# Eight-tile cross-attention and ternary FFN kernel: transposes of p moved to DMA, shared scale steps, new engine orders

## The reference, cut to what matters

```python
def xattn(h, ctx, Wq, bq, Wk, bk):            # h = layernorm(x)
    q, k = ctx @ Wq.T + bq, ctx @ Wk.T + bk
    return einsum('bln,bmn->blm', h, softmax(q @ k.T))
def bit_linear(x, w, b):
    sx = 127 / clip(max|x| per row);  xq = clip(round(x*sx), -128, 127) / sx
    gw = clip(mean|w|);               wq = clip(round(w/gw), -1, 1) * gw
    return xq @ wq.T + b
x = x + xattn(layernorm(x), ...)
h = layernorm(x)
p = silu(bit_linear(h, gate_w, gate_b)) * bit_linear(h, val_w, val_b)   # 256 -> 1024
x = x + bit_linear(p, out_w, out_b)                                     # 1024 -> 256
```

## Time and profile before

| | us |
|---|---|
| median of 3 runs (65.54 to 68.28) | 65.64 |
| the profiled execution's own time | 64.93 |
| its span in the trace | 63.1 |
| TensorE / VectorE / ScalarE / GpSimd busy | 51.7 / 48.1 / 48.7 / 47.5 |
| bytes moved by DMA | 7.20 MB |

### The profile page before, as it was taken

One profiled execution on the slowest core, in us unless ns is written; L12 is line 12 of the kernel. 1 busy time (PEld: TensorE's weight loads), 2 busy tenths in 40 slices (PEclk: granted clock), 3 DMA queues, 4 the chain that ended last, 5 costly groups with the idle time before them and its releaser, 6 DMA issues.

```text
span 63.1 us, 1253 instructions
## 1 busy us (share of the span) xinstructions
PE 51.7 (82%) x348; PEld 34.5 (55%) x352; DVE 48.1 (76%) x134; ACT 48.7 (77%) x89; POOL 47.5 (75%) x98
## 2 busy tenths in 40 slices
PE   2999998985898957772979899999999999699400
PEld 1758876855686545122326434565457477589200
DVE  4300469998989899999989798999999957946500
ACT  0806799999999969977996954799899899995000
POOL 4359821759898985978797789899999999979200
PEclk9999999999999999999999999999999999999997
DMA  0888999999996100000000000000000000022643
GB/s 0 212 190 238 385 420 308 308 418 367 358 354 250 45 0 0 10 5 5 0 0 0 0 0 0 0 0 10 0 0 0 0 0 0 0 83 95 215 151 130
DMA packets 4102, 7.20 MB, mean 114 GB/s; under 512 B 472, under 2 KB 2300, under 8 KB 4096
## 3 DMA queue, kind: packets, MB, share of 16 engines
q1 hardware_dynamic: 3944, 6.99, 32.8%
q10 hardware_dynamic: 152, 0.14, 0.7%
HBM read 6.04 MB, written 1.05 MB: 112 GB/s over the span
## 4 chain that ended last, share of the span: by engine, by line
PE 50%; POOL 19%; DVE 9%; issue 8%; DMA 5%; ACT 2%; POOLq 0%; ACTq 0%
PE psG L776 10%; PE psO L852 9%; PE psV L803 7%; PE psT L823 5%; DMA wqk_sb<-in_wqk 5%; POOL res L334 4%; POOL w_int L363 4%; PE psG L791 4%; DVE nmax L403 3%; PE psH L852 3%; POOL prob L283 3%; PE psG L690 3%; PE psT L705 3%; POOL rstd L293 2%; DVE st L396 2%
## 5 line engine op out<-in xcount | busy, mean ns | idle before, releaser
L632 ACT ACTIVATE sil<-psG,s_gv 128x1024 f32<-128x1024 f32 x8 | 8.9, 1118 | 2.0 <-PE psG L791 1.9
L514 DVE TENSOR_REDUCE pmax<-prod 128x1 f32<-128x1024 f32 x8 | 9.6, 1208 | 0.0
L501 DVE TENSOR_TENSOR prod<-psV,sil 128x1024 f32<-128x1024 f32 x7 | 8.5, 1218 | 0.7 <-ACT sil L632 0.3
L776 PE MATMUL psG<-ter_gate,hT 128*128 128x512 bf16 x29 | 7.7, 378 | 1.1 <-ACT sil L632 0.6
L349 POOL TENSOR_SCALAR prod<-prod,pqs 128x1024 f32<-128x1024 f32 x7 | 7.8, 1120 | 0.3 <-DVE pqs L527 0.3
L641 ACT ACTIVATE pT<-psT,unshift 128x1024 bf16<-128x1024 f16 x7 | 7.8, 1118 | 0.1
L803 PE MATMUL psV<-ter_val,hT 128*128 128x512 bf16 x27 | 7.0, 380 | 0.1
L403 DVE TENSOR_REDUCE nmax<-psT 128x2 f32<-128x512 f32 x4 | 2.7, 684 | 5.6 <-PE psT L705 5.6
L852 PE MATMUL psO<-ter_out,pT 128*128 128x256 bf16 x48 | 6.2, 273 | 0.5 <-ACT o_early L649 0.5
L852 PEld LDWEIGHTS psO<-ter_out,pT 128*128 128x128 bf16 x48 | 4.4, 98 | 1.5 <-issue 0.9
L776 PEld LDWEIGHTS psG<-ter_gate,hT 128*128 128x128 bf16 x32 | 2.7, 96 | 3.8 <-issue 1.7
(11 more groups left out here) (135 smaller groups left out, 142.7 us busy)
## 6 DMA issues: line engine op xcount, KB each, us to landing
x<-in_x_tok SPq DMA_DIRECT2D x4, 256.0 KB, 6.7
xt_sb<-in_x_T SPq DMA_DIRECT2D x4, 256.0 KB, 6.6
w_gate<-in_w_gate SPq DMA_DIRECT2D x2, 512.0 KB, 6.8
w_val<-in_w_val SPq DMA_DIRECT2D x2, 512.0 KB, 9.2
w_out<-in_w_out SPq DMA_DIRECT2D x2, 512.0 KB, 6.6
out_x<-res SPq DMA_DIRECT2D x8, 128.0 KB, 1.8
ctx_sb<-in_ctx_T SPq DMA_DIRECT2D x2, 128.0 KB, 3.0
ctx_sb<-in_ctx_T SPq DMA_DIRECT2D x1, 256.0 KB, 4.6
```

The costliest lines, as they stand in the source:

```text
L501: nc.vector.tensor_tensor(prod[:, t % P_RING, :], psV[:], sil[:, t % S_RING, :], ALU.mult).then_inc(prod_done, 1)
L514: nc.vector.tensor_reduce(pmax[:, t:t + 1], prod[:, t % P_RING, :], AX.X, ALU.max, apply_absolute_value=True).then_inc(pmax_done, 1)
L632: nc.scalar.activation(sil[:, t % S_RING, :], psG[:], ACT.Silu, scale=s_gv[:, t, 0:1]).then_inc(sil_done, 1)
L776: nc.tensor.matmul(psG[:, c * HC:(c + 1) * HC], hT[:, t, k, :], w_ter[0][:, k * HID + c * HC:k * HID + (c + 1) * HC], start=(k == 0), stop ...
```

## The change

**p of tiles 0 to 5.** `p_round_int` writes the rounded p as int16 to a ring of four (`p_int`); GpSimd does tiles 0 and 3, ScalarE 1, 2, 4 and 5. SyncE issues a transposing DMA of 128x1024 (`turn`), and `widen` turns int16 into bf16: ScalarE for 0, 1, 4, 5, VectorE for 2, 3. Tiles 6 and 7 keep TensorE's transposes; `p_copy(6)` is VectorE's, both halves of tile 7 are copied by ScalarE.

**Scale steps.** Groups of tiles (0,1), (2,3) and (4 to 7) in place of four pairs. `inverse_parts` is GpSimd's for all groups; rT of the last two groups comes by transposing DMAs (`turn_r`). `hstep` and most of `gamma_p` are GpSimd's.

**Bias rows.** `bias_parts` is VectorE's; TensorE spreads the three parts with a selection matrix (`bias_spread`, three products of 512 columns into psO), ScalarE copies them (`bias_copy`). The nine DMAs are gone.

**Loads and orders.** The contexts and b_out are laid out in HBM as they are read. All of x, both halves of the gate weights and the first half of the value weights are loaded ahead of x transposed. `q_out` 1 to 3 are VectorE's, `normalise` 0, 1 GpSimd's, 3 ScalarE's, `load_silu` stands ahead of `att_copy(2)`. All engine lists are new. The diff, cut:

```diff
+    NDMA = 6
+    H_PE = 8
+    GROUPS = ((0, 2), (2, 4), (4, 8))
...
-            def spread_bias():
-                sp.wait_ge(bh_step, 5)
-                sp.wait_ge(c_rows0, 2)
-                for r in range(KB):
-                    sp.dma_start(bias_rows[r:r + 97:32, :], bh_part[:, r % NPART, :]).then_inc(l_rows, 16)
+            def turn(t):
+                sp.wait_ge(pround_done[t], 1)
+                if t >= I_RING:
+                    sp.wait_ge(pT_sb[t - I_RING], 1)
+                sp.dma_start_transpose(pT_int[:, t % I_RING], p_int[:, t % I_RING, :]).then_inc(turned[t % I_RING], 16)
+            def turn_r(g):
+                a, e = GROUPS[g]
+                sp.wait_ge(r_step[g], 5)
+                sp.dma_start_transpose(rT[:, a:e], r_cols[:, a:e].rearrange("p t m -> p (t m)")).then_inc(rT_sb[g], 16)
...
-            load_ctx(0, 0, 1); load_ctx(1, 1, 2); load_ctx(2, 2, 4); load_x(0, 0, 2); load_x(1, 2, 4);
-            load_xt(0, 0, 1); load_w(0, 0); load_w(0, 1); load_bo(); load_x(2, 4, 6); load_x(3, 6, 8);
-            load_xt(1, 1, 2); load_w(1, 0); load_w(1, 1); spread_bias(); load_xt(2, 2, 3); load_w(2, 0);
-            load_w(2, 1); load_xt(3, 3, 4); store(0); store(1); store(2); store(3); store(4); store(5);
+            load_ctx(0, 0, 1); load_ctx(1, 1, 2); load_w(0, 0); load_x(0, 0, 2); load_w(0, 1);
+            load_ctx(2, 2, 4); load_x(1, 2, 4); load_x(2, 4, 6); load_x(3, 6, 8); load_w(1, 0);
+            load_xt(0, 0, 1); load_xt(1, 1, 2); load_bo(); load_w(1, 1); load_w(2, 0); load_xt(2, 2, 3);
+            load_w(2, 1); load_xt(3, 3, 4); turn_r(1); turn_r(2); turn(0); turn(1); turn(2); turn(3); turn(4);
+            turn(5); store(0); store(1); store(2); store(3); store(4); store(5); store(6); store(7)
...
+            def p_round_int(t):
+                act.wait_ge(pqs_done, t + 1)
+                if t >= I_RING:
+                    act.wait_ge(turned[t % I_RING], 16 * (t // I_RING))
+                nc.scalar.activation(p_int[:, t % I_RING, :], prod[:, t % P_RING, :], ACT.Copy,
+                                     scale=pqs[:, t:t + 1]).then_inc(pround_done[t], 1)
+            def widen(t):
+                act.wait_ge(turned[t % I_RING], 16 * (t // I_RING + 1))
+                if t >= T_RING:
+                    act.wait_ge(o_done, t - T_RING + 1)
+                nc.scalar.copy(pT[:, t % T_RING, :],
+                               pT_int[:, t % I_RING].rearrange("p k m -> p (k m)")).then_inc(pT_sb[t], 1)
...
+            k_out(0); q_out(0); abs_sum(0, 0); k_out(1); abs_sum(0, 1); exps(0); exps(1); k_out(2); bias_copy();
+            k_out(3); abs_sum(1, 0); att_copy(0); exps(2); att_copy(1); exps(3); abs_sum(1, 1); normalise(3);
+            load_silu(); att_copy(2); centre_x2(3); att_copy(3); to_int(0, 1); to_int(1, 0); to_int(1, 1);
+            h_copy(0); centre_x2(5); h_copy(1); centre_x2(6); centre_x2(7); silu(0); abs_sum(2, 0); h_copy(2);
+            silu(1); abs_sum(2, 1); h_copy(3); silu(2); h_copy(4); h_copy(5); silu(3); p_round_int(1);
+            h_copy(6); silu(4); p_round_int(2); widen(0); silu(5); widen(1); h_copy(7); scale_product(0);
+            silu(6); p_round_int(4); scale_product(1); p_round_int(5); silu(7); scale_product(2); widen(4);
+            scale_product(3); widen(5); p_round_half(0); scale_product(4); p_copy_half(0); p_copy_half(1)
...
+            def bias_spread():
+                pe.wait_ge(c_pick, 4)
+                pe.wait_ge(bh_step, 2 * NPART - 1)
+                for i in range(NPART):
+                    mm = nc.tensor.matmul(psO[:], pick16[:, i, :], bh_part[:, i, :], start=(i == 0),
+                                          stop=(i == NPART - 1))
+                mm.then_inc(rows_ps, 1)
```

More of the change, by code:

```diff
@@ L41, in xattn_ffn @@
     assert D == S == 256 and HC == 512 and NCH == 4 and KH * D == WN
-    S_RING, P_RING, T_RING = 3, 5, 3
+    S_RING, P_RING, T_RING, I_RING = 3, 5, 3, 4
     EARLY = 5
     LATE = 5
+    NDMA = 6
+    H_PE = 8
     LAST = T - 1
+    GROUPS = ((0, 2), (2, 4), (4, 8))
+    group = [g for g, (a, e) in enumerate(GROUPS) for _ in range(a, e)]
     WARM = 12
@@ L377, in _ @@
[L377 to L382 removed]
+                                        ALU.add).then_inc(early_done, 1)
@@ new lines, in _ @@
+            std_x(0, 2); normalise(0); normalise(1); to_int(0, 0); std_x(2, 4); std_x(4, 8); add_bias(0);
+            add_bias(1); centre_x2(0); centre_x2(1); std_x2(0); std_x2(1); h_step(0); gamma_h(0); h_step(1);
+            h_round(0); inverse_parts(0); centre_x2(4); h_round(1); h_round(2); gamma_h(1); std_x2(2);
+            inverse_parts(1); h_step(2); gamma_h(2); h_round(3); add_bias(2); h_round(4); h_round(5);
+            gamma_p(0); h_round(6); inverse_parts(2); gamma_p(1); p_round_int(0); add_bias(3); gamma_p(2);
@@ L561, in _ @@
-            p_max(5); gamma_p(4); gamma_p(5); times_value(6); invert_gamma_p(4); p_max(6); invert_gamma_p(5);
-            gamma_p(6); invert_gamma_p(6); times_value_half(0); times_value_half(1); p_max(7); gamma_p(7);
-            invert_gamma_p(7); p_round_half(1); add_residual(5); p_copy_half(1); add_residual(6);
-            add_residual(7)
+            bias_parts(); q_out(1); stats_x(0, 2); row_max(0); row_max(1); stats_x(2, 4); invert_sum(0);
+            q_out(2); invert_sum(1); gamma_w(0); stats_x(4, 6); scales_w(0); q_out(3); row_max(2);
@@ new lines, in _ @@
+            clip(1, 0); clip(1, 1); scales_h(1); h_max(2); times_value(0); p_max(0); h_inv(2); times_value(1);
+            scales_h(2); p_max(1); times_value(2); invert_gamma_p(0); p_max(2); invert_gamma_p(1); gamma_w(2);
+            times_value(3); scales_w(2); invert_gamma_p(2); p_max(3); times_value(4); clip(2, 0); clip(2, 1);
+            p_max(4); times_value(5); invert_gamma_p(3); p_max(5); invert_gamma_p(4); widen(2); gamma_p(5);
+            invert_gamma_p(5); times_value(6); p_max(6); widen(3); invert_gamma_p(6); times_value_half(0);
@@ L566, in _ @@
+            times_value_half(1); p_max(7); gamma_p(7); invert_gamma_p(7); p_round_half(1); p_copy(6);
+            add_residual(5); add_residual(6); add_residual(7)
         @block.scalar
@@ L663, in p_copy_half @@
                                      bias=unshift[:]).then_inc(pT_sb_half[i], 1)
-            k_out(0); q_out(0); k_out(1); q_out(1); q_out(2); exps(0); k_out(2); k_out(3); exps(1); q_out(3);
-            att_copy(0); abs_sum(0, 0); exps(2); abs_sum(0, 1); exps(3); centre_x2(0); centre_x2(1);
-            att_copy(1); att_copy(2); abs_sum(1, 0); abs_sum(1, 1); to_int(0, 0); centre_x2(2); centre_x2(3);
-            att_copy(3); to_int(1, 0); h_copy(0); abs_sum(2, 0); load_silu(); silu(0); h_copy(1); centre_x2(4);
-            centre_x2(5); centre_x2(6); centre_x2(7); h_copy(2); silu(1); abs_sum(2, 1); h_copy(3); silu(2);
-            h_copy(4); silu(3); h_copy(5); silu(4); to_int(2, 0); h_copy(6); p_copy(0); silu(5);
-            scale_product(0); h_copy(7); p_copy(1); silu(6); p_copy(2); scale_product(1); p_copy(3); silu(7);
-            scale_product(2); p_copy(4); p_copy(5); scale_product(3); p_copy(6); p_round_half(0);
-            scale_product(4); p_copy_half(0)
+            k_out(0); q_out(0); abs_sum(0, 0); k_out(1); abs_sum(0, 1); exps(0); exps(1); k_out(2); bias_copy();
[6 more added lines that the diff above has]
+            scale_product(3); widen(5); p_round_half(0); scale_product(4); p_copy_half(0); p_copy_half(1)
         @block.tensor
```

406 lines of the change are left out of this document (219 added, 187 removed).

## The result

The changed kernel takes 61.16 us (median of 4 runs, 60.71 to 61.61), 0.937 times the kernel before, 95% interval 0.930 to 0.944: 6.3% faster, where 2.9% was forecast. The time lies 0.54 us under the low end of the range. The profiled execution took 61.23 us around a span of 59.5 us. The kernel before has some longer executions (up to 68.28 us); the ratio leaves them out.

The account below looks back on a forecast made before the run. TensorE was taken as the feed-forward bound by a little, ScalarE next. Front +2.5, feed-forward -3.8, value(7) -0.6, tail 0 make -1.9: span 63.1 to 61.2, median 63.7 us (-2.9%), range 61.7 to 66.7.

Parts of the forecast that it names:

- Front, +2.5: Before feed-forward: ScalarE's added work and waits move the first rT copy from 23.21 to 25.7 us, 2.5 us later.
- the prediction's signs of being wrong: Profile signs against the forecast, among them abs_sum(0,0) starting at 6 or 9 us, or h_copy(0) past 27 us.
- Feed-forward, -3.8: First rT copy to last silu's end: 28.58 falls to 24.8 us, with ScalarE busy 23.0 and idle 1.8.
- the 1.2 us of cover: VectorE in feed-forward: done at 49.3 us, 1.2 us ahead of need; an edit beyond that would show at once.
- value(7) no longer late, -0.6: Start of the tail: times_value_half no longer waits 0.66 us after silu's end for TensorE's last value product.
- PE idle over 4 us: Sign of being right: TensorE idle for over 4 us in the feed-forward part.
- No stall at the turns: Transposing DMAs of p: each lands in 3.0 us, within the 2.9 to 3.0 us before widen, so no stall.
- The serial queue: Rival, chance 0.13: each transpose holds SyncE's queue for D us; gain gone at D 2.0, slower by 2% from 2.5.
- Tail, 0: From times_value_half to the end of the span: new ScalarE steps level with VectorE's, gain 0, ends -0.3 and +0.6.
- From span to median: Last step of the sum: span 61.2, profiled execution 63.0, median 0.71 above it, giving 63.7 us.
- front and idle both vanish: Rival, chance 0.12: gate-weight waits of 2.0 us go and feed-forward idle falls by another 1 us; 61.8 us.
- The others: Remaining rivals: transposes late 65.3 us (0.17), serial queue (0.13), front late 66.0 (0.08), nothing for TensorE about 66.6 (0.05).

Follow-up runs that it names:

- the doubled turns: Changed kernel with a second, unused transposing DMA of the same size behind each of turns 2 to 5: 63.24 us, ratio 0.970 to the kernel before.
- the late residuals: Changed kernel with GpSimd's residuals 1 to 4 behind the last output scales and the wait for the last rounding: 61.76 us, ratio 0.946 to the kernel before.

## Why the prediction was right and wrong

- **Front, +2.5: right** (+2.40), partly by luck. ScalarE's work was 18.32 us where 18.1 was counted, but the waits fell elsewhere: abs_sum(0,0), for which 1.5 us had been counted, started at 6.29 without a wait, one of the prediction's signs of being wrong, and abs_sum(0,1) waited 1.5 us where 0.5 was counted. What was added for GpSimd's steps was needed too: with the weights early the start stayed at 25.7.
- **Feed-forward, -3.8: right within 0.3** (-4.09). Busy 22.43 against 23.0, idle 2.06 against 1.8. VectorE did follow, but without the 1.2 us of cover that I gave it: it was free at 50.09, silu(7) ended at 50.10.
- **value(7) no longer late, -0.6: right** (-0.63), and shown by undoing: with p's transposes on TensorE it is 0.8 us late again. The forecast that TensorE would have 3 us to spare was wrong in size: 28.09 us of work for 27.6 counted, in 29.86, so 1.8 us. "PE idle over 4 us" did not come. Of the 2.2 us by which the span grows with the transposes back, the late value(7) is 0.8, the later silu 0.7 and the last store 0.9; the stretch between gives 0.2 back.
- **No stall at the turns: nearly right.** Landing 3.2 us for 3.0 taken. widen(3) and widen(4) waited 0.31 and 0.48 us for DMA, where none was forecast, and the tail up to the last residual still took 6.70 us for 6.7. The serial queue needed D over 1.4 us to hurt; D is 1.24, and the doubled turns show a loss beyond it, smaller than the rival's sum. The Trainium skill's 1309 ns for a block (VectorE: DVE Perf Modes, The three transpose paths) is not borne out as a sum of blocks, whose estimate was 10.5 us a tile; nor are its 350 to 400 GB/s (DMA: Bandwidth & Descriptors, Latency and other measured facts): with two turns under way the DMA engines moved 185 GB/s at a busy share of 0.97 (47.60 to 49.10 us), and 256 KB in 3.2 us from issue to landing are 82 GB/s. The measured landing decides.
- **Tail, 0: wrong, and the step that failed.** "Early stores leave sooner but the last sets the end" takes the last store as free to start when its residual is done. It was not: in the kernel before it started 1.24 us later, 0.53 us of it behind stores that had lined up on SyncE's queue and 0.71 by one issue of 1145 ns. Both went: -1.25 us. A row for it was in reach, since the stores' view gives a last start of 60.9 beside a last residual that ended at 59.66; I read the end of the span from the residual and never asked who issued the store. That lining up stores costs time is shown by the late residuals (0.7 us of queue). The long issue came and went with p's transposes on TensorE, in both orders; why it takes 0.8 to 2.2 us is open. A slip beside it: the prediction writes 55.78 - 52.45 for VectorE's 3.0 us, which is 3.33; the steps that it names take 3.0.
- **From span to median.** Of the 2.54 us between 63.7 and 61.16, the tail is 1.25, the front, feed-forward and value(7) together 0.42, the tail up to the last residual 0.03. The 0.71 us that I had added for the median's place above the profiled execution, 0.07 that the median now lies below it, and 0.06 of rounding are the rest: an offset of a few runs of the kernel before that did not carry over.
- **Rivals.** The nearest in time, "front and idle both vanish" (61.8), is not what happened: neither vanished, ScalarE idled for 2.2 us in the front and 2.1 in the feed-forward part. The others needed waits that the profile lacks.

## What to carry to other kernels

Follow the end of the span backwards from the last store, not from the last computation: what stands ahead of it on the issuing queue belongs to the tail, and a change that touches only the middle can free it. A slow but parallel path (a DMA of 3.2 us instead of 0.45 us on TensorE) pays only where the order of the consumers leaves that long between producer and use; the same transposes gained 2.4 us in one order and lost 1.6 us in the other. Whether an edit reached the program is told by the count of instructions in the trace. When a step is moved back on one engine, move back with it each waiter on the others, or everything queued behind that waiter is late.

## What was not expected of the hardware

- A DMA transpose's issue hardly depends on its size: 1.23 to 1.28 us for p's 128x1024 tile, 1.19 to 1.24 us for rT's 128x512 and 128x256, in the changed kernel; landing 3.2 and 2.4 us. A plain store's issue takes 0.33 to 0.57 us.
- One store in each of the four kernels with p's transposes on TensorE takes 0.83 to 2.19 us to issue, each time with a packet of the instruction queue at it or up to 1 us ahead; landings around it grow (up to 3.7 us). One DMA transpose at such a packet took 1.72 us.
- The same first loads, in the same order, made the gate weights usable at 6.22 us in one execution and at 7.28 us in another, on another chip, and ScalarE's front moved with them.
